# Building the slot map's one-hot tables block by block, and splitting the expert weights' conversion, in a four-layer kernel on one core

## The chip, the core and the metric

The kernel runs on one core of a Trainium2 chip. The core has five engines that matter here: TensorE (PE, matrix multiplies; PEld is its weight load), VectorE (DVE), ScalarE (ACT), GpSimd (POOL), and SyncE (SP), which issues most DMAs. Each engine takes its instructions in program order, and engines meet only at semaphores. The metric is the device time of one execution in microseconds (us), as the median of several runs.

## The reference, cut to what matters

The input x (8 sequences of 512 tokens, 256 features) passes through four residual layers: a cross attention, a transformer block whose feed-forward part is a mixture of eight experts, a second cross attention, and a gated feed-forward. The change touches the mixture of experts alone:

```python
top_w, top_i = jax.lax.top_k(probs, 2)
top_w = top_w / top_w.sum(-1, keepdims=True)
for e in range(8):
    gate_e = jnp.sum(jnp.where(top_i == e, top_w, 0.0), axis=-1)
    he = jax.nn.gelu(xf @ w1[e] + b1[e])
    out = out + gate_e[:, None] * (he @ w2[e] + b2[e])
```

Each of the 4096 tokens goes to two experts. w1[e] is 256 x 1024 and w2[e] is 1024 x 256, both float32, 1 MB each.

## The kernel before

The kernel runs eight phases one after the other, each ended by a barrier of all engines. The seventh, `phase_experts` (tiles with the prefix `ex_` in the trace), runs from about 1558 to 2070 us.

**Routing.** Tokens are not computed against all experts. Every (token, choice) pair gets a slot, slots of one expert are neighbours, and slots are cut into 39 tiles (`TILES`) of 256 (`TE`). VectorE computes `slot` for each pair: partition p and block n (`NT` is 32) name token n*128+p, and k in 0, 1 the choice. The map must then be turned round, from slot to token, and that is done by a matrix product of one-hot tables. `lo` is the slot modulo 128, `hi` the slot divided by 128. `at_lane[k]` (128 x 32 x 128, bf16) holds a one where the column is `lo`; `at_tile[k]` (128 x 32 x 2 x 78, bf16, with `HI` = 78) holds, where the column is `hi`, the block number n in plane 0 and the partition number in plane 1. For each k and n one matmul (L1429) multiplies the two, 64 in all, summed in `psH[0]`; VectorE then forms 128 times plane 0 plus plane 1, the token of each slot, as `token` (L1346 to L1349). In the kernel before, VectorE makes the ones of `hi` for all n at once (L1327), GpSimd multiplies them by n into plane 0 (L1257), VectorE makes `at_lane` for all n at once (L1330), waits for GpSimd, and multiplies plane 1 by the partition number (L1333). This goes k = 0, then k = 1.

**Gathers.** GpSimd waits for `token` and issues for each tile two indirect DMAs that fetch 128 rows each (L1267), up to two tiles ahead.

**Tiles.** Tile s works with expert `emap[s]`. TensorE transposes the rows of tile s (L1440), ScalarE copies them to `xT` (L1400, `transposed`). `hidden(s, f)` for f = 0 to 3 is 12 matmuls into `psH[f]` (L1452); ScalarE applies gelu to its two halves (L1410) and VectorE splits the result in two float16 parts (L1371, L1372). `output(s, f)` is 12 matmuls into `psY` (L1466). TensorE's order in tile s is hidden 0, output 2 of tile s-1, hidden 1, output 3 of tile s-1, transposes of tile s+1, hidden 2, output 0, hidden 3, output 1. After output 3 of tile s-1, VectorE copies `psY` out (`out_tile`, L1359 and L1360) and signals `y_free`, for which output 0 of tile s waits.

**Weights.** All experts' weights end up in SBUF as two float16 parts. For each expert e and half k (k = 0 is w1, k = 1 is w2) SP loads the float32 half into `stage[k]` (L1199), ScalarE writes the high part (`weights_high`, L1388), VectorE the low part (`weights_low`, L1341). There is one stage buffer per half, so the load of expert e+1's half waits on `w_ready` until the low part of expert e's half is done. Experts 0 and 1 (`AHEAD` = 2) are handled before the first tile, expert s+2 in tile s for s = 0 to 5: both halves at the end of the tile's work on ScalarE and on VectorE. On SP the body of tile s loads the 4 KB bias `b1` of tile s (L1212, `load`), stores tile s-2 (L1216, `store`), and then issues both halves of expert s+2. ScalarE waits for `b1` before the first gelu of its tile.

The first eight tiles are written out, the others run in a loop of two tiles.

Of the kernel before, what the change touches and what calls it, by code (L numbers as in the profile page):

```python
# [6 lines left out]
BF16 = mybir.dt.bfloat16  # L7
# [4 lines left out]
ALU = mybir.AluOpType  # L12
# [4 lines left out]
P = 128  # L17
B, S, D = 8, 512, 256
TT = S // P
DC = D // P  # L20
# [7 lines left out]
E_N, FF = 8, 1024  # L28
FC = FF // P
NT = B * TT  # L30
TE = 256
CHOSEN = 2
# [3 lines left out]
WSCALE = 64.0  # L36
# [1074 lines left out]
def phase_experts(nc, c, scr):  # L1111
# [7 lines left out]
    w1h = c.sb("w1h", [P, E_N, 2, DC, FF], F16)  # L1119
    w2h = c.sb("w2h", [P, E_N, 2, FC, D], F16)  # L1120
# [10 lines left out]
    HI = TILES * HALF  # L1131
# [3 lines left out]
    lo, hi = c.sb("lo", [P, CHOSEN, NT], BF16), c.sb("hi", [P, CHOSEN, NT], BF16)  # L1135
# [22 lines left out]
               for k in range(CHOSEN)]  # L1158
# [8 lines left out]
    (gr_in, set_done, sel_ready, cum_ps, slot_ready, slot_out, hot_ready, row_hot, chunk_hot, token_ps, token_ready,  # L1167
     hi_done, w_ready, own, x_ps, x_ready, h_ps, h_free, hl_ready, y_ps, y_free) = (
        c.sem(n) for n in ("gr_in", "set_done", "sel_ready", "cum_ps", "slot_ready", "slot_out", "hot_ready",
                           "row_hot", "chunk_hot", "token_ps", "token_ready",  # L1170
# [3 lines left out]
    AHEAD = 2  # L1174
# [11 lines left out]
    with nc.Block() as block:  # L1186

        @block.sync
        def _(sp):
# [3 lines left out]
            def weights(e):  # L1193
                for k in range(2):
                    if e > 0:
                        sp.wait_ge(w_ready, 2 * e + k - 1)
                    src = scr["w1"][e].rearrange("(c p) f -> p c f", p=P) if k == 0 else (
                        scr["w2"][e].rearrange("(c p) d -> p c d", p=P))
                    sp.dma_start(stage[k][:].rearrange("p (c f) -> p c f", c=DC if k == 0 else FC), src  # L1199
                                 ).then_inc(w_in[k], 16)  # L1200

            for e in range(AHEAD):
                weights(e)
            sp.wait_ge(slot_ready, 2)
            sp.dma_start(scr["slots"], slot[:]).then_inc(slot_out, 16)
            sp.dma_start(scr["gsel"], gsel[:]).then_inc(slot_out, 16)

# [11 lines left out]
            def body(s, q):  # L1219
                load(s, q)  # L1220
                if not (isinstance(s, int) and s < 2):
                    store(s - 2, q)
                if isinstance(s, int) and s + AHEAD < E_N:
                    weights(s + AHEAD)
# [9 lines left out]
        def _(pool):  # L1234
# [20 lines left out]
            for k in range(CHOSEN):  # L1255
                pool.wait_ge(hot_ready, k + 1)
                pool.tensor_tensor(at_tile[k][:, :, 0, :], at_tile[k][:, :, 1, :],  # L1257
                                   lane[:, 0:NT].unsqueeze(2).to_broadcast([P, NT, HI]), ALU.mult
                                   ).then_inc(chunk_hot, 1)
# [12 lines left out]
        def _(dve):  # L1272
# [63 lines left out]
            def weights_low(e):  # L1336
                for k, wh in enumerate((w1h, w2h)):
                    dve.wait_ge(hi_done, 2 * e + k + 1)
                    src = stage[k][:]
                    flat = wh[:, e].rearrange("p r c f -> p r (c f)")  # L1340
                    dve.scalar_tensor_tensor(out=flat[:, 1, :], in0=src, scalar=WSCALE, in1=flat[:, 0, :],  # L1341
                                             op0=ALU.mult, op1=ALU.subtract).then_inc(w_ready, 1)

            weights_low(0)
# [5 lines left out]
            for e in range(1, AHEAD):  # L1350
                weights_low(e)
# [13 lines left out]
            def body(s, q):  # L1365
# [10 lines left out]
                if isinstance(s, int) and s + AHEAD < E_N:  # L1376
                    weights_low(s + AHEAD)
# [6 lines left out]
        def _(act):  # L1384
            def weights_high(e):
                for k, wh in enumerate((w1h, w2h)):
                    act.wait_ge(w_in[k], 16 * (e + 1))
                    act.mul(wh[:, e, 0].rearrange("p c f -> p (c f)"), stage[k][:], WSCALE).then_inc(hi_done, 1)  # L1388

            for e in range(AHEAD):  # L1390
                weights_high(e)
# [12 lines left out]
            def body(s, q):  # L1404
# [9 lines left out]
                if isinstance(s, int) and s + AHEAD < E_N:  # L1414
                    weights_high(s + AHEAD)
# [4 lines left out]
        def _(pe):  # L1420
# [914 lines left out]
```

## Time and profile before

| | |
|---|---|
| median of 3 runs | 2572.62 us (2568.93 to 2573.91) |
| the profiled execution | 2570.51 us |
| its span (first to last instruction) | 2568.8 us |
| busy: PE, DVE, ACT, POOL | 2123.9, 1537.6, 1072.8, 305.5 us |
| mean granted TensorE clock | 0.907 of full speed |

Times in the rows below are us from the start of the span, durations are us unless marked ns. A row of the timeline begins with the start and the duration, then engine, line, operation, output and inputs, shapes, and how many instructions were merged in it; in square brackets stands how long the engine was idle before it, and what ended the idle time. Starts of neighbouring instructions on one engine can lie closer together than a duration, since they overlap.

### The profile page before, as it was taken

The page shows a single profiled execution, that of the slowest core. Times are in us where ns is not written, and L with a number is a line of the kernel's source. Part 1 is how long each engine was busy: PE and PEld are TensorE (multiplying, and loading weights), DVE is VectorE, ACT ScalarE, POOL GpSimd, SP SyncE. Part 2 cuts the span into 40 slices and gives each one's busy share as a digit, 9 for nine tenths or more (in the row PEclk, how much of TensorE's full clock was granted, in tenths as well). Part 3 has the DMA queues.
Part 4 walks back from the last instruction along what each step waited for, and adds up shares of the span by engine and source line. Part 5 has one row for each costly group of instructions (what it writes and reads, how often), then busy time and mean ns, then how long its engine had stood idle before and what let it go on. Part 6 is the DMA issues. An engine that isn't in the chain of part 4 may idle for free. (4 is left out here: it accounts for less than half of the span.)

```text
span 2568.8 us, 46558 instructions
## 1 busy us (share of the span) xinstructions
PE 2123.9 (83%) x14650; PEld 1301.6 (51%) x14651; DVE 1537.6 (60%) x3132; ACT 1072.8 (42%) x1974; POOL 305.5 (12%) x368
## 2 busy tenths in 40 slices
PE   7757999999499738999996772799999945899987
PEld 4412333333265414555554661678888823556555
DVE  5755777776156535666662875654444435676663
ACT  3414666666122214554552110543333313555552
POOL 1000000000100000000000003211111132111100
PEclk9958999999799958999998875899999977999999
DMA  6742333330346642333313542531111132111100
GB/s 206 267 120 68 92 88 95 86 87 18 116 138 222 212 125 73 105 102 96 103 52 95 182 133 70 190 108 50 47 43 49 41 108 76 42 42 49 49 9 17
DMA packets 194258, 248.83 MB, mean 97 GB/s; under 512 B 23985, under 2 KB 145994, under 8 KB 194114
## 3 DMA queue, kind: packets, MB, share of 16 engines
q1 hardware_dynamic: 186674, 228.05, 28.7%
q0 software_dynamic: 6816, 18.62, 2.6%
q8 instruction: 84, 1.38, 0.2%
q14 instruction: 60, 0.49, 0.1%
q10 hardware_dynamic: 624, 0.30, 0.1%
HBM read 155.57 MB, written 90.25 MB: 96 GB/s over the span
## 5 line engine op out<-in xcount | busy, mean ns | idle before, releaser
L734 ACT ACTIVATE a_prob<-a_psE 128x512 f32<-128x512 f32 (+3 forms) x1024 | 499.7, 518 | 506.4 <-PE a_psE L631 253.1
L615 PE MATMUL a_psS<-a_K,a_Q 97*128 97x512 bf16 (+3 forms) x1024 | 364.0, 361 | 114.7 <-DMA a_Q<-a_nrow 41.6
L767 DVE TENSOR_REDUCE a_nm<-a_psS 128x2 f32<-128x1024 f32 x256 | 313.1, 1225 | 135.6 <-PE a_psS L615 134.3
L628 PE MATMUL a_psE<-a_Q,a_K 100*128 100x512 bf16 (+3 forms) x1024 | 358.7, 353 | 33.5 <-DMA a_Q<-a_nrow 22.3
L764 DVE TENSOR_REDUCE a_nm<-a_psS 128x1 f32<-128x128 f32 (+3 forms) x512 | 238.4, 488 | 174.1 <-PE a_psS L618 171.9
L1466 PE MATMUL ex_psY<-ex_w2h,ex_hl 128*128 x1872 | 231.8, 274 | 12.5 <-DVEq L1361 12.4
L628 PEld LDWEIGHTS a_psE<-a_Q,a_K 100*128 100x128 bf16 x1024 | 103.4, 102 | 270.2 <-ACT a_prob L734 191.3
L1452 PE MATMUL ex_psH<-ex_xT,ex_w1h 128*128 128x256 f16 x1872 | 234.3, 276 | 3.3 <-ACT ex_xT L1400 2.1
L641 PE MATMUL a_psO<-a_prob,a_V 128*32 128x512 f32 (+3 forms) x2048 | 234.8, 531 | 1.4 <-ACT a_prob L734 1.4
L615 PEld LDWEIGHTS a_psS<-a_K,a_Q 97*128 97x128 bf16 x1024 | 104.1, 103 | 242.0 <-DVE a_nm L764 72.3
L1410 ACT ACTIVATE ex_hf<-ex_psH,ex_b 128x256 f32<-128x256 f32 x312 | 130.7, 470 | 223.8 <-PE ex_psH L1452 219.5
L1466 PEld LDWEIGHTS ex_psY<-ex_w2h,ex_hl 128*128 128x128 f16 x1872 | 181.1, 98 | 42.6 <-issue 20.8
L1452 PEld LDWEIGHTS ex_psH<-ex_xT,ex_w1h 128*128 x1872 | 181.9, 99 | 30.4 <-issue 7.4
L1371 DVE CAST ex_hl<-ex_hf 128x512 f16<-128x512 f32 x156 | 67.7, 434 | 215.2 <-ACT ex_hf L1410 214.4
L537 POOL TENSOR_TENSOR a_rcx<-a_rc,a_one 128x512 f32<-128x512 f32 x64 | 66.5, 1038 | 942.1 <-DVE a_rc L795 942.1
L1267 POOL DMA_INDIRECT ex_xt<-s_xfs,ex_token x78 | 78.5, 1007 | 353.0 <-PE ex_psX L1440 334.4
L618 PE MATMUL a_psS<-a_cmq,a_identb 128*128 128x128 bf16 x512 | 117.6, 231 | 0.0
L631 PE MATMUL a_psE<-a_cmk,a_identb 128*128 128x128 bf16 x512 | 114.6, 225 | 0.0
L1372 DVE TENSOR_TENSOR ex_hl<-ex_hf,ex_hl 128x512 f16<-128x512 f32 x156 | 108.3, 694 | 5.4
L1068 PE MATMUL t_psV<-t_wo,t_cin 128*128 128x256 f32 x256 | 70.7, 444 | 34.2 <-DMA t_cin<-s_o 19.9
L401 PE MATMUL t_psV<-t_wo,t_cin 128*128 128x256 f32 x256 | 68.1, 413 | 18.0 <-DMA t_cin<-s_o 18.0
L2080 PE MATMUL la_psG<-la_yT,la_wgate 128*128 128x512 f16 x288 | 72.0, 387 | 11.7 <-ACT la_yT L1953 11.7
(273 smaller groups left out, 3146.1 us busy)
## 6 DMA issues: line engine op xcount, KB each, us to landing
s_qk<-t_parts SPq DMA_DIRECT2D x64, 384.0 KB, 3.2
s_v<-t_vaug SPq DMA_DIRECT2D x16, 1024.0 KB, 6.4
a_V<-s_v SPq DMA_DIRECT2D x64, 256.0 KB
s_o<-a_on SPq DMA_DIRECT2D x64, 256.0 KB, 2.1
t_cin<-s_o SPq DMA_DIRECT2D x16, 1024.0 KB, 8.6
ex_stage<-in_w SPq DMA_DIRECT2D x16, 1024.0 KB, 6.7
a_K<-s_qk SPq DMA_DIRECT2D x64, 192.0 KB
a_Q<-s_qk SPq DMA_DIRECT2D x64, 192.0 KB
```

What stands on the lines that cost most here:

```text
L615: last = pe.matmul(bank[:, 0:n], Q6[s][0:K_MAX, h, t * P:(t + 1) * P], K6[s][0:K_MAX, h, 0:n], start=True, stop=not causal)
L618: last = pe.matmul(bank[:, t * P:n], identb[:], cmq[:], start=False, stop=True)
L628: last = pe.matmul(bank[:, 0:S - q0], K6[s][0:K_EXP, h, t * P:(t + 1) * P], Q6[s][0:K_EXP, h, q0:S], start=True, stop=not causal)
L631: last = pe.matmul(bank[:, 0:P], identb[:], cmk[:], start=False, stop=True)
L641: last = pe.matmul(psO[h * HP:(h + 1) * HP, q0:S], V[s][:, t, h * HP:(h + 1) * HP], prob[(t * GH + h) % NP_BUF][:, 0:S - q0], start=t == 0 ...
L734: act.activation(prob[j % NP_BUF][:, 0:n], psE[j % NE][:, 0:n], ACT.Exp).then_inc(p_ready, 1)
L764: dve.tensor_reduce(nm[s % NM_BUF][:, t, h:h + 1], psS[j % NS][:, 0:n], axis=AX.X, op=ALU.max, negate=True).then_inc(s_free, 1)
L767: dve.tensor_reduce(nm[s % NM_BUF][:, t - 1:t + 1, h], psS_all[:, (j - 1) % NS:j % NS + 1, :], axis=AX.X, op=ALU.max, negate=True).then_in ...
L1372: dve.tensor_tensor(hl[q][:, 1, two, :], hf[:, two, :], hl[q][:, 0, two, :], ALU.subtract).then_inc(hl_ready, 1)
L1410: act.activation(hf[:, f, :], psH[f // 2][:, f % 2, :], ACT.Gelu_apprx_tanh, bias=b1[q][:, f:f + 1], scale=1.0 / (WSCALE * XSCALE)).then_i ...
L1452: last = pe.matmul(psH[f][:, j, :], w1h[:, ds(e, 1), wp, d, fc * P:(fc + 1) * P].rearrange("p o f -> p (o f)"), xT[q][:, xp * DC + d, :], ...
L1466: last = pe.matmul(psY[t][:, 0:D], hl[q][:, hp, fc, t * P:(t + 1) * P], w2h[:, ds(e, 1), wp, fc, :].rearrange("p o d -> p (o d)"), start=f ...
```

## The change

Four edits, all in `phase_experts`:

1. GpSimd's multiplication and the three wide VectorE operations per k go. In their place VectorE runs, for each k and each block n, three `tensor_scalar` operations: `at_lane` (128 columns, compared with the per-partition scalar `lo`), plane 0 of `at_tile` (78 columns, compared with the scalar `hi` and multiplied by the constant n), and plane 1 (78 columns, compared with `hi` and multiplied by the scalar `row`). `lo` and `hi` become float32. TensorE waits for each block's tables rather than for each k's.
2. VectorE's `weights_low` of expert 0 moves behind the computation of `token`.
3. `weights`, `weights_high` and `weights_low` take one half at a time. In tile s, ScalarE makes the first half's high part after the first gelu pair (f = 1) and the second's after the third pair (f = 5); VectorE makes the first half's low part after f = 1 (behind `out_tile`) and the second's after f = 3.
4. SP issues the stores of `slot` and `gsel` ahead of expert 1's weights, and the first half of expert 2 ahead of the loop of tiles. In tile s it issues the second half of expert s+2 and the first half of expert s+3.

```diff
-            for e in range(AHEAD):
-                weights(e)
+            weights(0, 0)
+            weights(0, 1)
             sp.wait_ge(slot_ready, 2)
             sp.dma_start(scr["slots"], slot[:]).then_inc(slot_out, 16)
             sp.dma_start(scr["gsel"], gsel[:]).then_inc(slot_out, 16)
+            weights(1, 0)
+            weights(1, 1)
+            weights(2, 0)
...
                 if isinstance(s, int) and s + AHEAD < E_N:
-                    weights(s + AHEAD)
+                    weights(s + AHEAD, 1)
+                if isinstance(s, int) and s + 1 + AHEAD < E_N:
+                    weights(s + 1 + AHEAD, 0)
...
             for k in range(CHOSEN):
-                dve.tensor_tensor(at_tile[k][:, :, 1, :], hi[:, k, :].unsqueeze(2).to_broadcast([P, NT, HI]),
-                                  lane[:, 0:HI].unsqueeze(1).to_broadcast([P, NT, HI]), ALU.is_equal
-                                  ).then_inc(hot_ready, 1)
-                dve.tensor_tensor(at_lane[k], lo[:, k, :].unsqueeze(2).to_broadcast([P, NT, P]),
-                                  lane[:].unsqueeze(1).to_broadcast([P, NT, P]), ALU.is_equal)
-                dve.wait_ge(chunk_hot, k + 1)
-                dve.tensor_scalar(at_tile[k][:, :, 1, :], at_tile[k][:, :, 1, :], row[:, 0:1], None, ALU.mult
-                                  ).then_inc(row_hot, 1)
...
-            weights_low(0)
+                for n in range(NT):
+                    dve.tensor_scalar(at_lane[k][:, n, :], lane[:], lo[:, k, n:n + 1], None, ALU.is_equal)
+                    dve.tensor_scalar(at_tile[k][:, n, 0, :], lane[:, 0:HI], hi[:, k, n:n + 1], float(n),
+                                      ALU.is_equal, ALU.mult)
+                    dve.tensor_scalar(at_tile[k][:, n, 1, :], lane[:, 0:HI], hi[:, k, n:n + 1], row[:, 0:1],
+                                      ALU.is_equal, ALU.mult).then_inc(chunk_hot, 1)
...
-            for e in range(1, AHEAD):
-                weights_low(e)
+            for e in range(AHEAD):
+                weights_low(e, 0)
+                weights_low(e, 1)
...
-                if isinstance(s, int) and s + AHEAD < E_N:
-                    weights_low(s + AHEAD)
+                    if f % 2 == 1 and isinstance(s, int) and s + AHEAD < E_N:
+                        weights_low(s + AHEAD, f // 2)
...
-                if isinstance(s, int) and s + AHEAD < E_N:
-                    weights_high(s + AHEAD)
+                    if f in (1, 5) and isinstance(s, int) and s + AHEAD < E_N:
+                        weights_high(s + AHEAD, f // 4)
...
             for k in range(CHOSEN):
-                pe.wait_ge(row_hot, k + 1)
                 for n in range(NT):
+                    pe.wait_ge(chunk_hot, k * NT + n + 1)
```

## Rows read from the trace of the kernel before

**Rows 1.** Busy time by stretch: PE, PEld, DVE, ACT, POOL, then PE clock, DMA share, GB/s.

```profile
1631.40:1644.40 13.00, 10.99 (x106) 9.65 (x104) 9.42 (x13) 7.85 (x11) 2.03 (x2) 1.00 0.61 203
1657.50:1672.30 14.80, 12.79 (x108) 10.59 (x106) 9.55 (x13) 7.85 (x11) 2.03 (x2) 0.88 0.55 177
```

**Rows 2.** Waits, 1555 to 1720 us: engine and line waited for, total, times, longest.

```profile
PE ex_psY L1466 <- DVEq L1361: 12.0, 6, 2.0
```

**Rows 3.** Timeline of VectorE, from the one-hot tables to the token list.

```profile
1574.63 2.76 DVE L1327 TENSOR_TENSOR ex_w1h<-ex_hi,ex_lane 128x2496 bf16<-128x2496 bf16 x1
...
1585.97 0.87 DVE L1333 TENSOR_SCALAR ex_w1h<-ex_w1h,ex_row 128x2496 bf16<-128x2496 bf16 x1 [4.25 <-POOL ex_w1h L1257]
1586.75 2.75 DVE L1327 TENSOR_TENSOR ex_w2h<-ex_hi,ex_lane 128x2496 bf16<-128x2496 bf16 x1
...
1598.87 2.29 DVE L1341 SCALAR_TENSOR_TENSOR ex_w1h<-ex_stage,ex_w1h 128x2048 f16<-128x2048 f32 x1
...
1603.33 0.24 DVE L1346 COPY ex_token_p<-ex_psH 128x78 f32<-128x78 f32 x1
...
1603.88 0.20 DVE L1349 CAST ex_token<-ex_token_f 128x78 uint32<-128x78 f32 x1
```

**Rows 4.** Timeline of TensorE, second table product, first tile, start of tile 1.

```profile
1599.01 4.28 PE L1429 MATMUL ex_psH<-ex_w2h,ex_hl 128*128 128x156 bf16 x32 [7.78 <-DVE ex_w2h L1333]
...
1614.72 5.30 PE L1452 MATMUL ex_psH<-ex_xT,ex_w1h 128*128 128x256 f16 x24 [2.06 <-ACT ex_xT L1400]
...
1625.68 1.47 PE L1452 MATMUL ex_psH<-ex_xT,ex_w1h 128*128 128x256 f16 x12
```

**Rows 5.** Groups by line and shape, VectorE: busy us, mean ns, idle us.

```profile
L964 DVE TENSOR_SCALAR t_y<-t_xres,t_mv,t_rstd 128x256 f32<-128x256 f32 x32 | 11.0, 408 | 11.4 <-POOL t_rstd L89 11.4
...
L1280 DVE TENSOR_SCALAR ex_second<-ex_gr 128x256 f32<-128x256 f32 x1 | 0.3, 289 | 0.0
...
L1307 DVE TENSOR_SCALAR ex_start<-ex_start 128x8 f32<-128x8 f32 x1 | 0.2, 171 | 0.0
```

**Rows 6.** Timeline of VectorE, four operations with two per-partition scalars each.

```profile
1411.06 1.38 DVE L964 TENSOR_SCALAR t_y<-t_xres,t_mv,t_rstd 128x256 f32<-128x256 f32 x4 [1.42 <-POOL t_rstd L89]
```

**Rows 7.** Timeline of ScalarE, expert 1's high parts and the first tile.

```profile
1606.21 1.91 ACT L1388 ACTIVATE ex_w1h<-ex_stage 128x2048 f16<-128x2048 f32 x1 [36.66 <-DMA ex_stage<-in_w]
1610.65 1.91 ACT L1388 ACTIVATE ex_w2h<-ex_stage 128x2048 f16<-128x2048 f32 x1 [2.52 <-DMA ex_stage<-in_w]
1612.71 1.01 ACT L1400 COPY ex_xT<-ex_psX 128x1024 f16<-128x1024 f16 x1 [0.15 <-PE ex_psX L1440]
...
1618.85 0.84 ACT L1410 ACTIVATE ex_hf<-ex_psH,ex_b 128x256 f32<-128x256 f32 x2
```

**Rows 8.** Timeline of SP's queue, the issues of expert 1's two halves.

```profile
1601.18 2.57 SPq L1199 DMA_DIRECT2D ex_stage<-in_w  x2
```

**Rows 9.** DMA issues between 1612 and 1617 us: KB, us from issue to landing.

```profile
ex_stage<-in_w SPq DMA_DIRECT2D x1, 1024.0 KB, 5.9
...
ex_b<-in_b SPq DMA_DIRECT2D x1, 4.0 KB, 4.9
```

**Rows 10.** Timeline of ScalarE in tile 1: last gelu pair and both weight halves.

```profile
1637.67 0.84 ACT L1410 ACTIVATE ex_hf<-ex_psH,ex_b 128x256 f32<-128x256 f32 x2 [3.95 <-PE ex_psH L1452]
1638.39 1.91 ACT L1388 ACTIVATE ex_w1h<-ex_stage 128x2048 f16<-128x2048 f32 x1
1640.20 1.91 ACT L1388 ACTIVATE ex_w2h<-ex_stage 128x2048 f16<-128x2048 f32 x1
```

**Rows 11.** Timeline of VectorE in tile 1: split of a pair, out_tile, later pairs.

```profile
1632.71 0.42 DVE L1371 CAST ex_hl<-ex_hf 128x512 f16<-128x512 f32 x1
...
1633.84 0.41 DVE L1359 TENSOR_SCALAR ex_yo<-ex_psY 128x256 f32<-128x256 f32 x1
...
1634.70 0.43 DVE L1371 CAST ex_hl<-ex_hf 128x512 f16<-128x512 f32 x1
...
1638.54 0.43 DVE L1371 CAST ex_hl<-ex_hf 128x512 f16<-128x512 f32 x1 [2.68 <-ACT ex_hf L1410]
```

More of the change, by code:

```diff
@@ L1134, in phase_experts @@
     lo_i, hi_i = c.sb("lo_i", [P, CHOSEN, NT], U32), c.sb("hi_i", [P, CHOSEN, NT], U32)
-    lo, hi = c.sb("lo", [P, CHOSEN, NT], BF16), c.sb("hi", [P, CHOSEN, NT], BF16)
+    lo, hi = c.sb("lo", [P, CHOSEN, NT]), c.sb("hi", [P, CHOSEN, NT])
     token_p, token_f = c.sb("token_p", [P, HI]), c.sb("token_f", [P, HI])
@@ L1165, in phase_experts @@
     PRODUCTS = ((0, 0), (0, 1), (1, 0))
-    (gr_in, set_done, sel_ready, cum_ps, slot_ready, slot_out, hot_ready, row_hot, chunk_hot, token_ps, token_ready,
+    (gr_in, set_done, sel_ready, cum_ps, slot_ready, slot_out, chunk_hot, token_ps, token_ready,
      hi_done, w_ready, own, x_ps, x_ready, h_ps, h_free, hl_ready, y_ps, y_free) = (
-        c.sem(n) for n in ("gr_in", "set_done", "sel_ready", "cum_ps", "slot_ready", "slot_out", "hot_ready",
-                           "row_hot", "chunk_hot", "token_ps", "token_ready",
+        c.sem(n) for n in ("gr_in", "set_done", "sel_ready", "cum_ps", "slot_ready", "slot_out", "chunk_hot", "token_ps", "token_ready",
                            "hi_done", "w_ready", "own", "x_ps", "x_ready", "h_ps", "h_free", "hl_ready",
@@ L1191, in _, with weights @@
                          scr["gates"].rearrange("b p t r e -> p b (t r e)")).then_inc(gr_in, 16)
[L1193 to L1200, printed above, removed]
-            for e in range(AHEAD):
-                weights(e)
+            def weights(e, k):
+                if e > 0:
+                    sp.wait_ge(w_ready, 2 * e + k - 1)
+                src = scr["w1"][e].rearrange("(c p) f -> p c f", p=P) if k == 0 else (
+                    scr["w2"][e].rearrange("(c p) d -> p c d", p=P))
+                sp.dma_start(stage[k][:].rearrange("p (c f) -> p c f", c=DC if k == 0 else FC), src
+                             ).then_inc(w_in[k], 16)
+            weights(0, 0)
+            weights(0, 1)
             sp.wait_ge(slot_ready, 2)
@@ L1253, in _ @@
             pool.memset(grid[:, 0:1], -1.0).then_inc(set_done, 1)
[L1255 to L1259, printed above, removed]
             pool.wait_ge(token_ready, 1)
@@ L1326, in _, with weights_low @@
             for k in range(CHOSEN):
-                dve.tensor_tensor(at_tile[k][:, :, 1, :], hi[:, k, :].unsqueeze(2).to_broadcast([P, NT, HI]),
-                                  lane[:, 0:HI].unsqueeze(1).to_broadcast([P, NT, HI]), ALU.is_equal
-                                  ).then_inc(hot_ready, 1)
-                dve.tensor_tensor(at_lane[k], lo[:, k, :].unsqueeze(2).to_broadcast([P, NT, P]),
-                                  lane[:].unsqueeze(1).to_broadcast([P, NT, P]), ALU.is_equal)
-                dve.wait_ge(chunk_hot, k + 1)
-                dve.tensor_scalar(at_tile[k][:, :, 1, :], at_tile[k][:, :, 1, :], row[:, 0:1], None, ALU.mult
-                                  ).then_inc(row_hot, 1)
[L1336 to L1342, printed above, removed]
-            weights_low(0)
+                for n in range(NT):
[4 more added lines that the diff above has]
+                                      ALU.is_equal, ALU.mult).then_inc(chunk_hot, 1)
+            def weights_low(e, k):
+                dve.wait_ge(hi_done, 2 * e + k + 1)
+                flat = (w1h, w2h)[k][:, e].rearrange("p r c f -> p r (c f)")
+                dve.scalar_tensor_tensor(out=flat[:, 1, :], in0=stage[k][:], scalar=WSCALE, in1=flat[:, 0, :],
+                                         op0=ALU.mult, op1=ALU.subtract).then_inc(w_ready, 1)
             dve.wait_ge(token_ps, 1)
@@ L1384, in _, with weights_high @@
         def _(act):
[L1385 to L1388, printed above, removed]
+            def weights_high(e, k):
+                act.wait_ge(w_in[k], 16 * (e + 1))
+                act.mul((w1h, w2h)[k][:, e, 0].rearrange("p c f -> p (c f)"), stage[k][:], WSCALE).then_inc(hi_done, 1)
             for e in range(AHEAD):
-                weights_high(e)
+                weights_high(e, 0)
+                weights_high(e, 1)
             act.wait_ge(token_ready, 1)
```

## The prediction

> **What bounds the kernel now.** Phases are divided by barriers, so only the expert phase can change, and a microsecond gained or lost there passes to the end one to one. I read the stretches first, then who waits for whom, then the timelines of each engine through the two places that the edits touch.
>
> The first place is the entry, from the one-hot tables to the first tile. TensorE has nothing else to do, so the path is VectorE's: tables from 1574.63 to 1598.87, of which 4.25 us per k are idle for GpSimd, then expert 0's low parts while TensorE runs the second product, then the token list at 1603.33 [rows 3, 4]. Next come the gather, expert 1's weights, the copy of the first rows at 1612.71 and the first hidden product at 1614.72 [rows 4, 7]. ScalarE's copy of the first rows stands in its queue behind expert 1's second high part (1610.65 + 1.91) and was idle only 0.15 us before it [rows 7]: two paths, rows and weights, arrive together.
>
> The second place is tiles 1 to 6. TensorE is 10.99 busy of 13.00 us, and idles 2.0 us before output 0, six times, 12.0 in all, waiting for `out_tile`, which VectorE reaches late because both low parts ran ahead of it [rows 1, 2]. So a tile takes 13.09 with the stall and 11.08 without. In two of these tiles the granted clock fell from 2.4 to 1.2 GHz for a while, right after such an idle, and the tile took 14.8 instead of 13.1: 1.7 us each; one of the two is among [rows 1]. From tile 7 on there is no such stall, and nothing that the change touches.
>
> **Part 1, the tables.** Removed: 24.24 us (1574.63 to 1598.87). Added: 192 small operations. Their price is the distance from start to start. I write it as c + p x (scalars read per partition) + columns.
> The scalar: L964 lasts 408 ns with two of them, L1280, the same shape with a constant, 289 ns, so p = 0.060 [rows 5]. The columns: L1280 against L1307, 8 columns in 171 ns, gives 0.48 ns per f32 column and 0.167 us for an operation of none [rows 5]; L1333, 2496 bf16 columns and one scalar, lasts 0.87, so 0.645 is left for columns, 0.26 ns each [rows 3]. The rest: the operation after L1333 starts 0.78 behind it, so c + p = 0.135 [rows 3]; four of L964 span 1.38 with 0.408 for the last, so 0.324 apart, less 0.123 for columns is c + 2p = 0.201 [rows 5, 6]. With p = 0.060 these give c = 0.075 and 0.081; I take 0.075, from the row of the same type. Then `at_lane` costs 0.075 + 0.060 + 0.033 = 0.168, plane 0 0.155, plane 1 0.215: 0.539 per block before rounding, 64 x 0.539 = 34.5 us. That is more than the 24.2 removed; what GpSimd's absence saves is eaten by 256 scalar reads (15.4 us of the 34.5).
>
> The trace has no bf16 `tensor_scalar` of 78 columns. Below: if scalars were free for such forms, 64 x 0.299 = 19.1 us. Above: if the 78 columns ran at half rate, +2.6 us; if each operation had to end before the next starts (0.227 and 0.287 plus columns), 52.2 us. I take 34.5, since p comes out of durations and of starts alike.
>
> The Trainium skill, page "VectorE: DVE Perf Modes", section on the TRN2 errata, prices an SBUF operation at 58 cycles plus columns over rate and has no term for scalars. By it the tables would take an estimated 64 x 0.256 = 16.4 us, and the change would come out some 10 us faster than the kernel before. The rows contradict it by 60 ns per scalar; its case is the first rival.
>
> TensorE's products now run behind each block and only the last counts, some 0.35 us in place of 4.3. The last table operation starts at 1574.63 + 34.5 - 0.2 = 1608.9 and ends 0.3 later; the token list starts at 1609.6 instead of 1603.33, 6.3 later.
>
> **Part 2, expert 0's low parts behind the token list.** They start 0.66 after the list begins, 1610.3 instead of 1598.87: 11.4 later. They free the stages, so expert 1's loads, its high parts and the first rows' copy queued behind them on ScalarE also move by up to 11.4 [rows 7, 8]. The gather needs tokens only 6.3 later and is hidden behind that. The loads collide less with the gather and no longer with the slot stores, so the second half may land sooner after the first than the 4.4 us of rows 7, though not closer than the 1.9 that ScalarE needs for the first; I take 10.9, bounds 9.9 to 11.4. Bias 0 is now issued behind expert 2's first half; it lands 9.2 to 10.1 us after expert 1's first high part starts (1.91 + 2.29 for the high and the low part, 5.0 to 5.9 for the load) and the first gelu comes some 3.4 + 8.2 = 11.6 after it [rows 3, 7, 9]: hidden, with about 1.5 us to spare.
>
> **Part 3, halves split, and part 4, SP's order.** With VectorE's `out_tile` ahead of the low part, the old stall goes. What is late next is the load. Expert s+2's first half may be issued only when `stage[0]` is free, that is after the low part of expert s+1, now in the middle of tile s-1. And SP issues bias s behind that megabyte. In rows 9 a 4 KB bias issued behind one half landed 4.9 us after its own issue, together with the half's 5.9. So ScalarE can't start tile s until about 5.1 after the low part's end (1601.18 to 1606.21 is 5.03 for a half, rows 7, 8). From there the chain closes on itself: load and bias 5.15; gelu pair 0.72; high part 1.81; second pair to its split 0.87; split 1.13; `out_tile` 0.86; low part 2.29 [rows 3, 10, 11]. Sum 12.83 us per tile, against the 11.08 that TensorE needs. Output 0 still waits for `y_free`, now because the gelu ahead of it is late: 1.75 us per tile for tiles 2 to 5.
> Tile 0, counted from its first gelu: the second pair starts at 0.72 + 1.81 = 2.53, its split ends at 4.5, the low part at 6.8, bias 1 lands at 11.9; through the same steps `y_free` comes at 17.4. TensorE starts tile 1 at 6.83, as before (1618.85 to 1625.68, rows 4 and 7), and reaches output 0 some 7.0 later (five of its eight blocks and the transposes), at 13.9. So 3.5 us in tile 1. Tile 6 has neither late bias nor weights. Total 3.5 + 4 x 1.75 = 10.5 us in place of 12.0: a gain of 1.5. Clock falls follow idles of the same length but there are five, placed otherwise; I take one of 1.7 us instead of two (bounds none, two). The second half has slack: issued at the end of the tile's VectorE work, it lands about when ScalarE ends the third pair.
>
> **The sum.** +10.9 - 1.5 - 1.7 = +7.7 us. The profiled execution, 2570.51 with a span of 2568.8, becomes 2578.2. The median of the runs shown lies 2.1 above that execution, so I forecast 2580.3.
>
> **The rivals.**
> - Scalars are free (part 1 at 19.1 us): 15.4 less, net -7.7, 2564.9 us. Against it: rows 3, 5 and 6. Break-even for the whole change is a table stage of 26.8 us (34.5 - 7.7); below it the change is faster. 10%.
> - Bias s isn't delayed behind the megabyte. Then only the high part waits for the load, the chain loses 0.83 (12.0), five times: net +3.5, 2576.1, no difference. Against it: 4.9 us for 4 KB. 8%.
> - Operations one after another at full duration (52.2): net +25.4, 2598 us. Against it: starts in rows 3 and 6 lie closer than durations. 7%.
> - The splits do what they say and all 12.0 us and both clock falls go (the load lands in time): net 10.9 - 15.4 = -4.5, 2568.1, within 0.2% too. For it: the load had slack before; against it: it is now issued some 7 us later relative to its use. 3%.
>
> The main case, 72%: its own range comes from a landing of 5.9 instead of 5.1 (+4.8 over five tiles and the entry), half rate for 78 columns (+2.6), and the entry and clock bounds: +4 to +16.
>
> About 0.2% (5.1 us) is what a measurement here can tell from no change. Of the main case some 55% lies above +5.1 and 17% within. With the rivals: slower 55 + 7 = 62%, same 17 + 8 + 3 = 28%, faster 10%. The range leaves out the free scalars and the serial case and takes in the others: 2568 to 2589.
>
> **What would show each step.** Table operations about 0.17, 0.16 and 0.21 us apart, the stage 34 us long, token list near 1609.6. First hidden product near 1625.6. In tiles 2 to 5, ScalarE's first gelu released by the bias's DMA, not by TensorE, and TensorE idle about 1.8 before output 0; hidden 0 starts 12.8 apart. If tiles 1 to 6 take 11.1 each, the load argument is wrong; if the stage takes under 20 us, the price of a scalar is.

## The result and the profile after

The changed kernel is slower: 2581.43 us as the median of 12 runs (2575.61 to 2588.43), against 2573.79 for the kernel before, run on the same chip in turns (12 runs, 2568.93 to 2580.63). The ratio of runs taken side by side is 1.0032, with a 95% interval of 1.0019 to 1.0045, or about 8.2 us. The forecast was 2580.3 us, and slower by over 0.2% was its likeliest case.

The profiled execution of the changed kernel took 2580.78 us with a span of 2579.0, 10.2 longer than the span before. I cut both at three marks: the first table operation, the last group of products of the expert tiles (L1466 before, L1460 after), and the end. Up to the first mark the kernel after is 2.1 us shorter (1572.55 against 1574.63), in phases that the change doesn't touch. From there to the last products of the expert tiles, called the expert stretch below, it takes 499.49 us against 489.73, that is 9.8 more. What follows is 2.5 longer. Only the 9.8 lie where the change is, and they compare one trace of each kernel.

The tables on VectorE, three operations per block (start, duration, engine, line, operation, tiles and shapes; next, the end of the stage):

```profile
1572.55 0.25 DVE L1326 TENSOR_SCALAR ex_hl<-ex_lane,ex_lo 128x128 bf16<-128x128 bf16 x1
1572.72 0.24 DVE L1327 TENSOR_SCALAR ex_w1h<-ex_lane,ex_hi 128x78 bf16<-128x78 bf16 x1
1572.87 0.30 DVE L1329 TENSOR_SCALAR ex_w1h<-ex_lane,ex_hi,ex_row 128x78 bf16<-128x78 bf16 x1
1573.08 0.25 DVE L1326 TENSOR_SCALAR ex_hl<-ex_lane,ex_lo 128x128 bf16<-128x128 bf16 x1
...
1605.90 0.30 DVE L1329 TENSOR_SCALAR ex_w2h<-ex_lane,ex_hi,ex_row 128x78 bf16<-128x78 bf16 x1
1606.61 0.24 DVE L1339 COPY ex_token_p<-ex_psH 128x78 f32<-128x78 f32 x1 [0.41 <-PE ex_psH L1423]
...
1607.28 2.29 DVE L1335 SCALAR_TENSOR_TENSOR ex_w1h<-ex_stage,ex_w1h 128x2048 f16<-128x2048 f32 x1
```

The starts lie 0.17, 0.15 and 0.21 us apart, though an operation lasts 0.24 to 0.30. The token list begins 34.06 us after the first table operation; before it was 28.70 [rows 3].

ScalarE from expert 1's high parts into tile 1, in the same columns:

```profile
1614.44 1.91 ACT L1381 ACTIVATE ex_w1h<-ex_stage 128x2048 f16<-128x2048 f32 x1 [46.26 <-DMA ex_stage<-in_w]
1618.78 1.91 ACT L1381 ACTIVATE ex_w2h<-ex_stage 128x2048 f16<-128x2048 f32 x1 [2.43 <-DMA ex_stage<-in_w]
1620.60 0.99 ACT L1394 COPY ex_xT<-ex_psX 128x1024 f16<-128x1024 f16 x1
...
1626.71 0.84 ACT L1404 ACTIVATE ex_hf<-ex_psH,ex_b 128x256 f32<-128x256 f32 x2
...
1638.61 0.84 ACT L1404 ACTIVATE ex_hf<-ex_psH,ex_b 128x256 f32<-128x256 f32 x2 [4.36 <-DMA ex_b<-in_b]
1639.34 1.91 ACT L1381 ACTIVATE ex_w1h<-ex_stage 128x2048 f16<-128x2048 f32 x1
1641.14 0.84 ACT L1404 ACTIVATE ex_hf<-ex_psH,ex_b 128x256 f32<-128x256 f32 x2
```

The first gelu comes 54.16 us after the first table operation, against 44.22 before [rows 3, 7]. In tile 1 ScalarE waits 4.36 us for a bias of 4 KB, and then makes the high part ahead of the second gelu pair. Before, it waited for TensorE there [rows 10].

The waits from 1555 to 1720 us (who waits, for whom, total, times, longest), and TensorE at output 0 of tile 1:

```profile
ACT ex_hf L1404 <- DMA ex_b<-in_b: 21.3, 5, 5.4
...
PE ex_psY L1460 <- DVEq L1355: 11.8, 4, 3.4
```

```profile
1639.41 1.47 PE L1446 MATMUL ex_psH<-ex_xT,ex_w1h 128*128 128x256 f16 x12
1644.09 1.47 PE L1460 MATMUL ex_psY<-ex_w2h,ex_hl 128*128 x12 [3.21 <-DVEq L1355]
```

TensorE still loses 11.8 us ahead of output 0 where it lost 12.0 [rows 2]. The idles are 3.21, 2.10, 3.06, 0.16 and 3.40 us in tiles 1 to 5, in place of six of 2.0. From the first gelu to the transposes of the ninth group, the stretch that holds the tiles with weight work, the kernel takes 93.98 us, and before it took 93.96.

So by these two traces the whole loss lies ahead of the first tile, and the edits to the tiles neither give nor take.

### The profile page after: what moved, and what is told of

It reads as the page before. It is cut to its first block and busy times, and to the rows that moved or that the text cites. A ratio compares the mean times of both kernels' runs of the same rounds, so it can differ in the third digit from the quotient of the medians.

```text
span 2579.0 us, 46740 instructions
## 1 busy us (share of the span) xinstructions
PE 2130.0 (83%) x14650; PEld 1297.6 (50%) x14651; DVE 1555.0 (60%) x3318; ACT 1071.5 (42%) x1974; POOL 289.5 (11%) x366
## 5 line engine op out<-in xcount | busy, mean ns | idle before, releaser
L1460 PE MATMUL ex_psY<-ex_w2h,ex_hl 128*128 x1872 | 230.3, 273 | 12.4 <-DVEq L1355 12.2
L1460 PEld LDWEIGHTS ex_psY<-ex_w2h,ex_hl 128*128 128x128 f16 x1872 | 180.9, 98 | 42.3 <-issue 21.2
L1366 DVE TENSOR_TENSOR ex_hl<-ex_hf,ex_hl 128x512 f16<-128x512 f32 x156 | 108.0, 693 | 5.4
```

The lines of the kernel that those rows point to most:

```text
L1460: last = pe.matmul(psY[t][:, 0:D], hl[q][:, hp, fc, t * P:(t + 1) * P], w2h[:, ds(e, 1), wp, fc, :].rearrange("p o d -> p (o d)"), start=f ...
```

## The experiments

Each run was timed beside the kernel before, so its ratio is to that; the median of the kernel before lay between 2567.7 and 2573.8 us in the four sets of runs, so medians of different sets are not to be subtracted. One trace was kept of each kernel. For what happens inside the expert phase I give three distances from its trace: list and gelu, from the first table operation to the token list and to the first gelu, and tiles, from the first gelu to the transposes of the ninth group. The kernel before has 28.70, 44.22 and 93.96; the one after has 34.06, 54.16 and 93.98.

### The two halves of the change alone

The first run keeps the changed tables and low parts and goes back to the old weights schedule, on all three engines:

```diff
                 if isinstance(s, int) and s + AHEAD < E_N:
-                    weights(s + AHEAD, 1)
-                if isinstance(s, int) and s + 1 + AHEAD < E_N:
-                    weights(s + 1 + AHEAD, 0)
+                    weights(s + AHEAD)
...
+                if isinstance(s, int) and s + AHEAD < E_N:
+                    weights_high(s + AHEAD, 0)
+                    weights_high(s + AHEAD, 1)
```

> The tables block by block, with expert 0's low parts behind the token list, and the weight halves scheduled as in the kernel before. My theory: the two places are independent. From the first table operation to the first gelu it takes about 54 us as in the changed kernel (44.2 before), and tiles 1 to 6 look as before (six idles of 2.0 us): in all 9 to 10 us slower than the kernel before. Rival: the late loads of the split schedule feed back into the entry, and without them the entry is shorter; then 4 to 7 us slower.

Measured: 2580.17 us, ratio 1.0040 (1.0025 to 1.0056). List 34.06, gelu 54.37, tiles 94.11 with the same six idles of 2.0:

```profile
PE ex_psY L1458 <- DVEq L1351: 12.0, 6, 2.0
```

That is 10.3 us slower, against 9 to 10 expected. The tables with the moved low parts carry the whole loss.

The second run does the opposite: the old tables, expert 0's low parts ahead of the token list, and the changed schedule of weights.

```diff
+            weights_low(0, 0)
+            weights_low(0, 1)
             dve.wait_ge(token_ps, 1)
...
-            for e in range(AHEAD):
+            for e in range(1, AHEAD):
                 weights_low(e, 0)
```

> The weight halves split and SP's new order, with the tables and expert 0's low parts as in the kernel before. My theory: the old idle before output 0 is exchanged for an equal one, from the load of the next half to the gelu; four or five idles of 2 to 3.5 us in tiles 1 to 5, from the first gelu to the start of tile 7 about 88.7 us (before 88.7), total within 2 us of the kernel before. Rival, the recorded sum: loads land 5.1 us after their issue, idles sum to 10.5 us, one clock fall less: 3.2 us faster. Rival, the purpose of the split: idles gone, 12 to 15 us faster.

Measured: 2566.92 us, ratio 0.9985 (0.9972 to 0.9998). List 28.69, gelu 42.30, tiles 89.97. That is 1.9 us less at the entry and 4.0 less in the tiles. My own theory had no gain in the tiles; five idles remain, 8.4 us in sum, and the recorded sum (3.2 us faster) came nearest, with 3.9. ScalarE at the entry:

```profile
1605.46 1.91 ACT L1391 ACTIVATE ex_w1h<-ex_stage 128x2048 f16<-128x2048 f32 x1 [36.01 <-DMA ex_stage<-in_w]
1608.46 1.91 ACT L1391 ACTIVATE ex_w2h<-ex_stage 128x2048 f16<-128x2048 f32 x1 [1.09 <-DMA ex_stage<-in_w]
```

The two high parts are 3.0 apart, in place of 4.4 [rows 7], and that is most of the 1.9. In this run the 32 KB stores of the slots are issued at 1573.57, long before expert 1's halves, where the kernel before issues them right behind the halves. But the stores aren't shown to be the reason: the two runs with other wide tables below keep the old order and have their halves 3.2 and 3.1 apart. So the gain at the entry may be chance in the one trace of the kernel before, and only the 4.0 in the tiles are put down to the schedule. The two halves of the change don't add up, +10.1 and -5.1 by the expert stretch of the traces against +9.8 for both; the tile part is 4.0 us worse once the tables are changed too. First halves land later there than here (5.1 to 6.7 us against 4.8 to 5.2, see the landings below).

### The price of a per-partition scalar

```diff
-                    dve.tensor_scalar(at_tile[k][:, n, 1, :], lane[:, 0:HI], hi[:, k, n:n + 1], row[:, 0:1],
+                    dve.tensor_scalar(at_tile[k][:, n, 1, :], lane[:, 0:HI], hi[:, k, n:n + 1], 1.0,
                                       ALU.is_equal, ALU.mult).then_inc(chunk_hot, 1)
```

> The changed kernel with the constant 1.0 in place of the per-partition scalar row in plane 1; the plane then lacks the partition number, and the rows gathered are others. If a scalar read costs 60 ns from start to start, the 64 operations of plane 1 take 0.15 instead of 0.21 us, the stage 29.7 instead of 33.5 us, and the first gelu comes 3.8 us sooner after the first table operation. If the price lies in the second arithmetic operation or in the size, nothing moves.

Measured, one execution: 2579.93 us; list 30.15 instead of 34.06, so 3.91 us for 64 scalars, 61 ns each. The first gelu comes 3.2 us sooner (50.99), not 3.8, since expert 1's halves landed 5.1 apart. The rows of plane 1 (L1329) now start like those of plane 0 (L1327):

```profile
1571.65 0.24 DVE L1327 TENSOR_SCALAR ex_w1h<-ex_lane,ex_hi 128x78 bf16<-128x78 bf16 x1
1571.80 0.24 DVE L1329 TENSOR_SCALAR ex_w1h<-ex_lane,ex_hi 128x78 bf16<-128x78 bf16 x1
1571.95 0.25 DVE L1326 TENSOR_SCALAR ex_hl<-ex_lane,ex_lo 128x128 bf16<-128x128 bf16 x1
```

The price of 60 ns, taken from two rows of 256 float32 columns, holds for 78 bf16 columns as well.

### Expert 0's low parts

```diff
+            weights_low(0, 0)
+            weights_low(0, 1)
             dve.wait_ge(token_ps, 1)
```

with the loop behind the token list starting at expert 1.

> The changed kernel with expert 0's low parts back in front of the token list. My theory: the path to the first tile runs over expert 1's weights, so the token list comes 4.1 us later after the first table operation, the gather is still hidden, expert 1's loads start 1.1 us sooner, and the first gelu moves by -1 to 0 us. Rival: the gather is the path; then the first gelu moves 2 to 4 us later.

Measured: 2577.33 us, ratio 1.0028 (1.0015 to 1.0040). List 37.88, low parts at 33.47, gelu 51.59, tiles 93.71. The token list comes 3.8 later than in the kernel after, and the first gelu 2.6 earlier, where I had expected at most 1. The low parts start only 1.3 earlier, so the move doesn't account for 2.6 by itself. ScalarE shows the rest:

```profile
1612.69 1.91 ACT L1383 ACTIVATE ex_w1h<-ex_stage 128x2048 f16<-128x2048 f32 x1 [45.05 <-DMA ex_stage<-in_w]
1615.67 1.91 ACT L1383 ACTIVATE ex_w2h<-ex_stage 128x2048 f16<-128x2048 f32 x1 [1.07 <-DMA ex_stage<-in_w]
```

The halves are 2.98 apart here and 4.34 in the kernel after, where GpSimd issues its first gather at 1607.66, ahead of both of expert 1's loads (1609.59 and 1611.79); here the first gather is issued at 1611.02, behind both. That the gathers hold up the second half is my reading of these times; no run isolated it. Over all traces it fits but for one: the seven kernels with the token list first have their halves 4.1 to 5.1 apart, and of the six with the low parts first five have 3.0 to 3.2, while the kernel before has 4.4. Weights, not tokens, were the later of the two paths at the entry, so putting the token list first delayed the path that decides.

### Why the tiles gain nothing

The theory on record was a ring: the bias stands behind a megabyte, ScalarE starts the tile late, and its high part then delays the second gelu pair. The first run issues each bias ahead of the megabyte.

```diff
             def body(s, q):
-                load(s, q)
+                if not (isinstance(s, int) and s + AHEAD <= E_N):
+                    load(s, q)
...
                     weights(s + AHEAD, 1)
+                    load(s + 1, 1 - q)
                 if isinstance(s, int) and s + 1 + AHEAD < E_N:
                     weights(s + 1 + AHEAD, 0)
```

Bias 0 goes ahead of expert 1's weights in the same way.

> The changed kernel with each tile's 4 KB bias issued ahead of the first half of the next expert instead of behind it. My theory: the bias holds up only one gelu pair, the high part waits for the same load anyway; the chain per tile gets 0.7 to 0.8 us shorter, the idles before output 0 stay (1 to 2.5 us each), in all 3 to 4 us faster than the changed kernel. Rival: the bias alone is what is late; the idles vanish, 12 to 15 us faster than the changed kernel.

Measured: 2576.55 us, ratio 1.0038 (1.0023 to 1.0053). Gelu 54.26, tiles 86.74, 7.2 less than after. The wait for the bias is gone, but idles of 2.17, 1.08, 2.07 and 1.08 stay, as my theory had it. The waits put three of them down to `out_tile`:

```profile
PE ex_psY L1463 <- DVEq L1358: 5.3, 3, 2.2
```

So the bias is a part of the cause and not the whole. The second run leaves the bias where it is and moves ScalarE's high parts behind the next gelu pair:

```diff
+                    if f in (3, 7) and isinstance(s, int) and s + AHEAD < E_N:
+                        weights_high(s + AHEAD, f // 4)
                     if f == 3 and not (isinstance(s, int) and s == TILES - 1):
                         transposed(s + 1, 1 - q)
-                    if f in (1, 5) and isinstance(s, int) and s + AHEAD < E_N:
-                        weights_high(s + AHEAD, f // 4)
```

> The changed kernel with ScalarE's high parts one gelu pair later: first half after the second pair, second half after the fourth. The bias stays behind the load. My theory: the high part no longer stands between the load and the second gelu pair; a bias landing 5.2 us after the low part leaves the second pair on time, one landing 6.9 us after leaves it 1.6 us late. Idles before output 0 sum to 0 to 4 us instead of 11.8, in all 9 to 14 us faster than the changed kernel. Rival: the late bias is the cause, the idles stay at 1.5 us or more each.

Measured: 2571.88 us, ratio 1.0005 (0.9990 to 1.0020), some 7 us below the ratio of the changed kernel, where 9 to 14 were expected. Tiles 83.90, 10.1 less than after; ScalarE still waits 13.9 us for the bias, and TensorE 6.1, more than the 0 to 4 expected:

```profile
ACT ex_hf L1404 <- DMA ex_b<-in_b: 13.9, 5, 3.2
...
PE ex_psY L1460 <- DVEq L1355: 6.1, 5, 1.6
```

The third run makes both edits.

```diff
+                    load(s + 1, 1 - q)
...
+                    if f in (3, 7) and isinstance(s, int) and s + AHEAD < E_N:
+                        weights_high(s + AHEAD, f // 4)
```

> Both: bias ahead of the load, high parts one pair later. My theory: no idle before output 0 above 0.3 us, no clock fall in tiles 1 to 7, from the first gelu to the start of tile 7 some 73.5 us instead of 88.7; 13 to 16 us faster than the changed kernel, so 5 to 8 us faster than the kernel before. Rival: VectorE or ScalarE become the bound of a tile, with some 12 us per tile; then 8 us faster than the changed kernel.

Measured: 2564.92 us, ratio 0.9987 (0.9976 to 0.9998), 3.3 us faster than the kernel before against 5 to 8 expected. Tiles 77.39, one tile of 11.41 and then 11.01 us each. No wait of TensorE ahead of output 0 is left, and the granted clock stays at 2.4 GHz (PE, PEld, DVE, ACT and POOL busy, clock, DMA share, GB/s):

```profile
1628.00:1704.00 76.00, 75.69 (x713) 67.01 (x711) 62.19 (x83) 51.37 (x77) 19.98 (x14) 1.00 0.57 185
```

Those two orders together are the cause of the idle: in tiles 1 to 6 it is 11.9 us in the kernel after, 6.4 and 6.1 with either mended, and none with both.

### How long a load takes to land

In the kernel after, DMA issues of a first half (KB, us from issue to landing), one stretch each around 1646, 1660 and 1686 us; in the last two the store of a tile is among the issues (it went out 1.5 and 1.9 us behind the load, in the first 2.3):

```profile
ex_stage<-in_w SPq DMA_DIRECT2D x1, 1024.0 KB, 5.3
...
ex_stage<-in_w SPq DMA_DIRECT2D x1, 1024.0 KB, 6.3
s_ys<-ex_yo SPq DMA_DIRECT2D x1, 256.0 KB, 5.5
...
ex_stage<-in_w SPq DMA_DIRECT2D x1, 1024.0 KB, 6.7
```

The store of 256 KB goes out right behind the bias. This run puts it behind the second half:

```diff
                 load(s, q)
-                if not (isinstance(s, int) and s < 2):
-                    store(s - 2, q)
                 if isinstance(s, int) and s + AHEAD < E_N:
                     weights(s + AHEAD, 1)
+                if not (isinstance(s, int) and s < 2):
+                    store(s - 2, q)
```

> The changed kernel with the 256 KB store of tile s-2 behind the second weight half of its tile instead of ahead of it, so that no store is issued right behind the first half and the bias. Theory: the loads that took 6.3 and 6.7 us shared their time with that store; without it they land after 5.0 to 5.4 us, output 0 starts every 12.7 to 12.9 us, and from the first gelu to the transposes of tile 8 it takes 89 to 92 us instead of 94.0. Rival: the spread comes from the gathers or from the memory; then loads of 6 us and more remain.

Measured, one execution: 2579.11 us, tiles 91.69. The loads land after 5.1, 5.2, 5.1, 5.0 and 5.4 us, and output 0 starts 13.10, 12.96, 12.95 and 13.24 apart (1642.08, 1655.18, 1668.14, 1681.09, 1694.33), where the ring of the prediction has 12.83. The idles of tiles 2 to 5 are 2.01, 1.87, 1.86 and 2.16, near the 1.75 of the prediction (the row below names three of the five idles, that of 3.76 in tile 1 among them; the other two are put down to a split, L1366):

```profile
PE ex_psY L1460 <- DVEq L1355: 7.9, 3, 3.8
```

In this one execution no load was late. That doesn't show the store to be the cause: in the kernel after itself, the load at 1673.61 has a store 1.5 us behind it and landed after 5.1 us; with the old tables and the store in the changed place, the loads landed after 4.8 to 5.2; and in the last version below, with the store only 0.4 behind, after 5.0 to 5.3. It was mostly one load, that of expert 5's first half, that was late: 6.3 in the kernel after, and 7.8, 8.1, 6.2, 6.0 and 8.0 in the runs with one scalar, low parts first, bias first, high parts late and both. In all six a store ran beside it. So a late load was seen only beside a store, and most loads beside a store weren't late. What decides between 5 and 8 us is left open.

### Other ways to make the tables

These two start from the kernel before. In the first, VectorE goes on with k = 1 while GpSimd multiplies k = 0, and makes plane 0 of k = 1 itself:

```diff
+            dve.wait_ge(chunk_hot, 1)
+            dve.tensor_scalar(at_tile[0][:, :, 1, :], at_tile[0][:, :, 1, :], row[:, 0:1], None, ALU.mult
+                              ).then_inc(row_hot, 1)
+            link(dve.tensor_tensor(at_tile[1][:, :, 0, :], at_tile[1][:, :, 1, :],
+                                   lane[:, 0:NT].unsqueeze(2).to_broadcast([P, NT, HI]), ALU.mult))
```

> The kernel before, with only the table work in another order: wide operations as before, both k's ones and at_lane first, GpSimd multiplies k = 0 alone, VectorE multiplies k = 1 itself, and the products with the partition number come last. VectorE then has no idle: 2.67 + 4.35 twice, 0.78, 2.67, 0.78: 18.3 us instead of 24.2. My theory: the path runs over VectorE's low parts and expert 1's loads, so all 5.9 us come through to the first gelu and to the end. Rival: the gather or ScalarE hold the first tile; then under 3 us.

Measured: 2568.80 us, ratio 0.9997 (0.9985 to 1.0009). Low parts at 22.99 (before 24.24), gelu 41.58, tiles 92.03. The stage shrank by 1.25 us, not by the 5.9 expected, though it had 8.5 us of waiting to hide [rows 3]; most of the other 1.4 of the 2.6 at the gelu is the halves' distance, 3.2 for 4.4. VectorE and GpSimd in that stage:

```profile
1572.69 4.42 DVE L1330 TENSOR_TENSOR ex_hl<-ex_lo,ex_lane 128x4096 bf16<-128x4096 bf16 x1
1577.04 6.91 DVE L1327 TENSOR_TENSOR ex_w2h<-ex_hi,ex_lane 128x2496 bf16<-128x2496 bf16 x1
```

```profile
1572.69 8.64 POOL L1257 TENSOR_TENSOR ex_w1h<-ex_w1h,ex_lane 128x2496 bf16<-128x2496 bf16 x1 [16.52 <-DVEq L1329]
```

GpSimd is issued at the same moment as L1330 of VectorE and ends at 1581.33, which is 4.2 us after L1330's end. VectorE's next operation, which takes 2.76 us elsewhere [rows 3], takes 6.91 and ends 2.6 after GpSimd. The two engines took turns. The Trainium skill, page "SBUF — State Buffer", section "SBUF: two separate sides", says that the pair of ports shared by the two is an exclusive lock, held for a whole instruction when a VectorE operation has two SBUF inputs and the GpSimd operation reads SBUF; this trace agrees in both directions, 4.4 us one way (GpSimd, until 1577.11) and 4.2 the other (6.91 less 2.76).

The second run gives up GpSimd. VectorE makes the four wide operations per k, plane 0 by a multiplication over all blocks:

```diff
-                dve.wait_ge(chunk_hot, k + 1)
+                link(dve.tensor_tensor(at_tile[k][:, :, 0, :], at_tile[k][:, :, 1, :],
+                                       lane[:, 0:NT].unsqueeze(2).to_broadcast([P, NT, HI]), ALU.mult))
```

> The kernel before, with GpSimd's multiplication done by VectorE in one wide operation per k, nothing else moved. Theory: GpSimd's 8.46 us are 4.3 of waiting while VectorE builds at_lane and 4.2 of work; the two never run side by side, so VectorE doing it in 2.7 us shortens each k from 12.1 to 10.5, the stage from 24.2 to 21.0, and the first gelu comes 3.2 us sooner after the first table operation. Rival: GpSimd's work was overlapped with at_lane and moving it adds 2.7 us of VectorE in place of a wait of 4.2: then the same 1.6 us per k. Both say so; what would contradict is a stage above 22 us. In all 2 to 4 us faster than the kernel before.

Measured: 2564.84 us, ratio 0.9992 (0.9981 to 1.0003). Low parts at 21.41, gelu 39.96, tiles 94.94 with three clock falls in place of two. The multiplication takes VectorE 2.75 us where the wait for GpSimd was 4.25, so the stage is 2.8 us shorter, near the 3.2 expected. The expert stretch is 3.4 us shorter; the interval of the ratio still includes no change. The first gelu came 4.3 sooner and not 2.8, as expert 1's halves, with SP's order as before, landed 3.08 apart and not 4.44:

```profile
1604.07 1.91 ACT L1383 ACTIVATE ex_w1h<-ex_stage 128x2048 f16<-128x2048 f32 x1 [33.10 <-DMA ex_stage<-in_w]
1607.15 1.91 ACT L1383 ACTIVATE ex_w2h<-ex_stage 128x2048 f16<-128x2048 f32 x1 [1.17 <-DMA ex_stage<-in_w]
```

The stage of 21.4 us is what the changed tables would have had to beat; they need 33.5 for the same stage (33.47 where the low parts follow them directly).

### A version with what held

The wide tables on VectorE alone, the low parts of expert 0 ahead of the token list, the bias ahead of the megabyte, the high parts behind the next gelu pair, SP's order of the change otherwise.

```diff
-                for n in range(NT):
-                    dve.tensor_scalar(at_lane[k][:, n, :], lane[:], lo[:, k, n:n + 1], None, ALU.is_equal)
...
+                link(dve.tensor_tensor(at_tile[k][:, :, 0, :], at_tile[k][:, :, 1, :],
+                                       lane[:, 0:NT].unsqueeze(2).to_broadcast([P, NT, HI]), ALU.mult))
...
+            load(0, 0)
+            weights(1, 0)
```

> The pieces that helped together: wide tables on VectorE alone, expert 0's low parts ahead of the token list, the slot stores and the biases ahead of the loads, ScalarE's high parts one gelu pair later than in the changed kernel. Theory: first gelu 39 us after the first table operation (44.2 before, 54.2 changed), 77.4 us from there to the transposes of tile 8 (94.0 in both): 20 to 22 us faster than the kernel before. Rival: with earlier tokens the gather or the loads hold the first tile; then the entry gains under 3 us and the whole 17 to 19.

Measured: 2549.70 us (6 runs, 2545.11 to 2554.29), ratio 0.9932 (0.9917 to 0.9948), some 17.5 us faster than the kernel before, where 20 to 22 were expected. Gelu 39.52 (-4.7) and tiles 77.40 (-16.6) came as expected, with the expert stretch at 469.28 (-20.5); the last phase took 3.7 us more than in the kernel before (486.0 against 482.2). TensorE through 76 us of tiles:

```profile
1620.00:1696.00 76.00, 76.00 (x719) 67.13 (x718) 58.99 (x81) 46.86 (x72) 21.89 (x14) 1.00 0.56 180
```

## Why the prediction was right, point by point

**Tables.** The starts were forecast 0.168, 0.155 and 0.215 us apart; they came 0.17, 0.15 and 0.21 apart, 0.524 per block against 0.539 (1572.87 to 1605.90 is 63 blocks), so 33.5 us for the 64 against 34.5. The constant was 0.069, not 0.075, which makes the 1 us. The token list is 5.4 later (forecast 6.3). Scalars cost 61 ns. The rival in which they are free falls. The Trainium skill, page "VectorE: DVE Perf Modes", section on the TRN2 errata, gives 58 cycles plus columns over rate, from which the estimate of 16.4 us was worked out: the trace has twice that. The rival of full durations one after another falls too, and so do the two rivals on the tiles: ScalarE waited 21.3 us for the bias, and 11.9 us of idle stayed.

**Entry.** Forecast +10.9, bounds 9.9 to 11.4, measured 9.94 (44.22 to 54.16). The mechanism held: loads released by the low parts, and ScalarE's copy behind the second high part. At 10.5 later for the low parts (34.73 against 24.24, forecast 11.4), the entry follows but for 0.5. I had hoped that the halves would land closer; they are 4.34 apart as before (4.44). What sets this distance isn't settled: without the slot stores it was 3.0 to 5.1 in the other runs, with them 3.1 to 4.5. As the kernel before is the only one with its low parts first and its halves over 3.3 apart, some 1.4 us of its entry may be chance, and the loss at the entry would then be over 11 us. The lower bound of 9.9 was not worked out either: halves 1.9 apart would have allowed 8.9. The run with the low parts first puts the cost of that step at 2.6 us, of which 1.3 are the earlier low parts and 1.4 the halves' distance.

**Tiles.** The idle in tile 1 was 3.21 (forecast 3.5), and the ring was seen: gelu released by the bias's DMA, 21.3 us in five times, and all idle gone when both of its parts were removed. The forecast of -3.2 for the tiles (-1.5 of idle, -1.7 of clock) didn't come; measured 0.0. The term that failed is the landing of load and bias, put at 5.15 from the low part's end to the gelu. It was 5.15 once, in tile 1, and 5.56, 6.49, 5.29 and 6.87 afterwards:

```profile
1643.95 2.29 DVE L1335 SCALAR_TENSOR_TENSOR ex_w1h<-ex_stage,ex_w1h 128x2048 f16<-128x2048 f32 x1
```

```profile
1651.80 0.84 ACT L1404 ACTIVATE ex_hf<-ex_psH,ex_b 128x256 f32<-128x256 f32 x2 [4.05 <-DMA ex_b<-in_b]
1665.92 0.84 ACT L1404 ACTIVATE ex_hf<-ex_psH,ex_b 128x256 f32<-128x256 f32 x2 [4.98 <-DMA ex_b<-in_b]
```

(The first of these gelus: 1651.80 less 1643.95 + 2.29 is 5.56.) Four tiles of 12.83 would take 51.3 us, and output 0 of tile 5 starts 54.75 after that of tile 1 (1644.09 to 1698.84). The 3.4 between them are about the four landings' excess over 5.15, 3.6 in sum. I took the 5.03 us of one load that had no store of 256 KB behind it, although the change puts one there, and kept the 5.9 of [rows 9] for the range only; that the store makes a load late isn't shown, as said above. The clock fell in two tiles as before (15.82 and 16.15 us long, behind idles of 3.06 and 3.40) and not in one.

**The sum.** +7.7 was forecast, made of +10.9 and -3.2. The trace has +9.8, of +9.9 and 0.0; the runs have +8.2 (4.9 to 11.6 by the interval). The entry came 1 us lower and the tiles 3.2 higher. These misses have opposite signs, and the total is off by less than the tiles are, 2.1 us in the trace and 0.5 in the runs: that it came so near is in part luck. Entry and total lie inside the ranges given.

**What stays open.** Beside the landings above, the phases behind the change. From the last phase's first product to the end the span takes 482.2 us before, 485.3 after and between 480.9 and 487.9 in the experiments, with no edit there. The three shortest are the kernel before and the two that start from it (480.9 to 482.5); all ten others have 484.0 and more. So the prediction's first step, that nothing changes outside the expert phase, isn't confirmed by these traces. It was 487.9 with the bias first and 486.7 with both tile edits, so a part of what these gain in the tiles may be lost again there: bias first is 7.2 us shorter in the tiles and yet no faster by its runs than the kernel after (1.0038 against 1.0032, intervals overlapping), where 3 to 4 us were expected; only its one traced execution is 5.5 us shorter. Whether it is the change that moves this phase or chance was not separated, since each kernel has one trace.

## What to carry to other kernels

Splitting one wide VectorE operation into many small ones with per-partition scalars has a price that can be read from the trace in advance: take the distance from start to start, not the duration, and add 60 ns for each scalar; here 192 small operations took 33.5 us where eight wide ones take 21.4. When two streams feed the start of a loop, find out which arrives last before one is moved ahead of the other. A small transfer that an engine waits for belongs ahead of a large one in the queue, and a helper's work (the high part) behind the operation that the critical engine needs next, not ahead of it; mending either order alone removed about half of the idle, and mending both all of it.

## What the runs showed of the hardware

GpSimd's multiplication of 2496 bf16 columns is recorded with 8.46 to 8.64 us, of which by my estimate only some 4.2 are work (what is left from the end of VectorE's two-input operation on): the rest is waiting for that operation to end. No run has GpSimd's multiplication alone. The same holds the other way round, where a VectorE operation of 2.76 us was recorded with 6.91. So in these traces the recorded duration of either engine includes its waiting for the other.

GpSimd's issue of an indirect DMA is longer too. It takes 0.95 us alone (the first 1.21), and 2.97 beside the low part, which has two SBUF inputs and runs from 1607.28 in the kernel after; in the kernel before, two issues beside low parts take 2.87 and 2.76:

```profile
1607.66 2.97 POOL L1265 DMA_INDIRECT ex_xt<-s_xfs,ex_token  x1 [48.88 <-DVE ex_token L1342]
1610.94 1.64 POOL L1265 DMA_INDIRECT ex_xt<-s_xfs,ex_token  x1 [0.30 <-issue]
1612.88 0.95 POOL L1265 DMA_INDIRECT ex_xt<-s_xfs,ex_token  x1 [0.30 <-issue]
```

In tiles 1 to 6 the granted clock fell from 2.4 to 1.2 GHz only behind an idle of TensorE ahead of output 0. The idles before a fall lasted 2.0 to 4.8 us, and 25 of the 43 idles of 2.0 us or more brought none. With no idle left (both tile edits, and the last version) it stayed at 2.4 GHz through them, and also where idles of 0.65 to 1.55 us were left (high parts late).
